# Second pass of an adaptive layer-norm block: the fourth pair's x2 is transposed by TensorE instead of by way of DRAM

## What is computed

```python
mod = (_silu(L0_c) @ L0_wmod).reshape(L0_c.shape[0], 6, 1, -1)
sa, ca, ga, sb, cb, gb = ...
h = _layernorm(x, axis=-1) * (1 + ca) + sa
x = x + ga * _L0_attn_ref(h, Wq, bq, Wk, bk, Wv, bv, Wo, bo)   # linear attention, 16 heads, elu + 1
h = _layernorm(x, axis=-1) * (1 + cb) + sb
x = x + gb * _L0_ffn_ref(h, ...)                              # value product + top 2 of 8 experts
return x                                                      # (1, 8192, 512), float32
```

## Time and profile before

| | us |
|---|---|
| runs, median of 3 (lowest to highest) | 1178.81 (1178.62 to 1179.45) |
| the profiled execution, its own time | 1178.39 |
| its span, first to last instruction | 1176.7 |
| PE busy / DVE / ACT / POOL | 1162.5 / 980.8 / 539.0 / 602.0 |
| granted TensorE clock, mean | 1.000 |

### The profile page before, as it was taken

One profiled execution on the slowest core, in us unless ns is written; L12 is line 12 of the kernel. 1 busy time (PEld: TensorE's weight loads), 2 busy tenths in 40 slices (PEclk: granted clock), 3 DMA queues, 4 the chain that ended last, 5 costly groups with the idle time before them and its releaser, 6 DMA issues.

```text
span 1176.7 us, 18181 instructions
## 1 busy us (share of the span) xinstructions
PE 1162.5 (99%) x5456; PEld 968.6 (82%) x5456; DVE 980.8 (83%) x2242; ACT 539.0 (46%) x1095; POOL 602.0 (51%) x458
## 2 busy tenths in 40 slices
PE   8999999999999999999999999999999999999998
PEld 5888888888887888888787788888888888888886
DVE  6998798888888988886788888888888888888875
ACT  4555545455445455545453443534435344344441
POOL 1444343433433433343564766666666666676632
PEclk9999999999999999999999999999999999999999
DMA  6566544543433434444313444443544534445321
GB/s 229 168 191 184 164 142 146 152 135 117 128 114 117 134 114 134 121 134 134 99 53 120 149 155 133 146 154 123 163 146 135 167 127 143 151 137 161 114 85 54
DMA packets 168834, 161.01 MB, mean 137 GB/s; under 512 B 16712, under 2 KB 115440, under 8 KB 168736
## 3 DMA queue, kind: packets, MB, share of 16 engines
q1 hardware_dynamic: 168736, 159.85, 43.6%
HBM read 95.30 MB, written 64.49 MB: 136 GB/s over the span
## 4 chain that ended last, share of the span: by engine, by line
PE 88%; DVE 4%; issue 2%; POOL 2%; ACT 2%; DMA 1%; SPq 0%; POOLq 0%; ACTq 0%; DVEq 0%
PE ps L1742 28%; PE ps L1743 28%; PE ps L1749 28%; PE ps L1963 1%; PE ps L1955 1%; POOL cn L759 1%; DMA wm_in<-in_L_wmod_dram 1%; PE ps L1850 1%; DMA q_in<-q_scratch 1%; PE ps L1761 0%; PE ps L1913 0%; PE ps L1918 0%; PE ps L1970 0%; DVE b2st L1282 0%; DVE b2st L1281 0%
## 5 line engine op out<-in xcount | busy, mean ns | idle before, releaser
L731 POOL TENSOR_TENSOR xn_lo<-xn,xn_hi 128x512 fp32r<-128x512 f32 x64 | 86.0, 1344 | 277.6 <-ACT xn_hi L866 277.6
L747 POOL TENSOR_TENSOR qks<-q_in,ks_q 128x1024 f32<-128x1024 f32 x32 | 76.9, 2403 | 103.6 <-DVE ws L1581 86.2
L759 POOL TENSOR_TENSOR cn<-c,half 128x16 f32<-128x16 f32 x32 | 93.6, 2926 | 36.9 <-DVE c L1499 36.9
L928 ACT CAST xT_hi<-ps 128x512 fp32r<-128x512 f32 x64 | 36.9, 577 | 154.3 <-DVE ps L1472 142.6
L875 ACT ACTIVATE exp_q<-qf 128x512 f32<-128x512 f32 x64 | 40.5, 633 | 141.1 <-DVE qf L1370 140.9
L1742 PE MATMUL ps<-wk_hi,xT_hi 128*128 128x512 f32 x256 | 100.4, 392 | 1.5 <-ACT xT_hi L860 1.4
L1742 PE MATMUL ps<-k_hi,xn_hi 128*128 128x512 f32 x256 | 101.9, 398 | 0.0
L1742 PE MATMUL ps<-wq_hi,xT_hi 128*128 128x512 f32 x256 | 101.3, 396 | 0.1
L1742 PE MATMUL ps<-g_hi,qT_hi 128*128 128x512 f32 x256 | 100.3, 392 | 0.1
L1742 PE MATMUL ps<-v_hi,xT_hi 128*128 128x512 f32 x256 | 100.2, 391 | 0.0
L1749 PE MATMUL ps<-k_hi,xn_lo 128*128 128x512 f32 x256 | 99.8, 390 | 0.0
(11 more groups left out here) (251 smaller groups left out, 3207.8 us busy)
## 6 DMA issues: line engine op xcount, KB each, us to landing
xin<-_attn_hidden_states_dram SPq DMA_DIRECT2D x64, 256.0 KB, 3.2
q_scratch<-qf SPq DMA_DIRECT2D x64, 256.0 KB, 3.3
xin<-_attn_hidden_states_dram SPq DMA_DIRECT2D x32, 512.0 KB, 4.3
q_in<-q_scratch SPq DMA_DIRECT2D x128, 128.0 KB, 3.0
out_dram<-qf SPq DMA_DIRECT2D x64, 256.0 KB, 2.3
xn_scratch<-xn SPq DMA_DIRECT2D x62, 256.0 KB, 2.0
xq<-xn_scratch SPq DMA_DIRECT2D x248, 64.0 KB, 2.5
x_scratch<-xn SPq DMA_DIRECT2D x56, 256.0 KB, 2.3
```

What stands on the lines that cost most here:

```text
L731: nc.gpsimd.tensor_tensor(moved(xn_lo[:, 1 - s, :], i + 1), kept(xn[:, 1 - s, :], i + 1), moved(f32(xn_hi[:, 1 - s, :]), i + 1), ALU.subtr ...
L747: nc.gpsimd.tensor_tensor(qks[:].rearrange("p h (g f) -> p (h g) f", f=P), q_of(j).rearrange("p (n f) -> p n f", f=P), ks_q[:].unsqueeze(1 ...
L759: nc.gpsimd.tensor_tensor(cn[:].rearrange("p h e -> p (h e)"), c2[:].rearrange("p h e -> p (h e)"), half[:], ALU.pow).then_inc(cn_done, 1)
L928: nc.scalar.copy(xT_hi[:, h, :], bank_x2T).then_inc(x2Th_done, 1)
```

## The change

`FIRST_TURNED` becomes 4, so that pair 3 is transposed by TensorE, and the way through DRAM begins with pair 4. The counts in the waits that had the 3 in them as a number are written with FIRST_TURNED, and the hand-written `turned_x2(3, 0)` on VectorE goes out. `turn_x2(3, 0)` and `turn_x2(3, 1)` appear on TensorE through `by_pe`; `normalised(3, ·)` writes `xn` without regrouping; SyncE's two stores and eight loads of pair 3 go out.

```diff
-        FIRST_TURNED, LAST_TURNED = 3, J - 2
+        FIRST_TURNED, LAST_TURNED = 4, J - 2
...
             def x2_load(j, h):
-                sp.wait_ge(x2_out[h], 16 * (j - 2))
-                wait_count(sp, x2T_turned, 2 * (j - 4) + h + 1)
+                sp.wait_ge(x2_out[h], 16 * (j - FIRST_TURNED + 1))
+                wait_count(sp, x2T_turned, 2 * (j - FIRST_TURNED - 1) + h + 1)
...
             def turned_x2(j, h):
-                dve.wait_ge(x2_back[h], 64 * (j - 2))
+                dve.wait_ge(x2_back[h], 64 * (j - FIRST_TURNED + 1))
...
             scores(2)
-            turned_x2(3, 0)
             weights(2)
             x2T_low(3, 0)
```

## The result

| | before | changed |
|---|---|---|
| runs, median of 6 each (lowest to highest), us | 1178.63 (1178.20 to 1179.45) | 1184.58 (1183.74 to 1185.06) |
| the profiled execution, its own time | 1178.39 | 1183.74 |
| its span | 1176.7 | 1182.0 |
| granted TensorE clock, mean | 1.000 | 0.997 |

The ratio is 1.0048, with a 95% interval of 1.0038 to 1.0058: slower by 5.9 us. The forecast was 1184.8 us. The profiled execution of the changed kernel is the quickest of its six.

The account below looks back on a forecast made before the run. TensorE's queue was taken to bound the kernel: −4.32 + 0.90 + 7.02 = +3.60 us, +6.0 with the restart, on 1178.39 is 1184.4, and 0.4 for the median gives 1184.8 us. Range 1181.9 to 1186.2.

Parts of the forecast that it names:

- The bound: TensorE, busy 1162.5 of 1176.7 us: the kernel ends when its queue of work and waits is done.
- The old stall: TensorE's delay at pair 3's products, where the transposed x2 came late by DRAM: all 4.32 us would go.
- The lower bound of 3.5: Least gain expected at pair 3's products, in us, as some delay might come back behind the new wait.
- Eight transposes: Pair 3's transposes added to TensorE's queue: 0.45 us a half, +0.90 us in all.
- The wait: TensorE at turn_x2(3, 1) waits for VectorE's x2T_low(3, 0), behind scores(2) and weights(2): +7.02 us.
- The restart: Matmuls behind TensorE's 7 us rest run slowly at first: +2.4 us, with 0 and 3.0 as ends.
- The sum: −4.32 + 0.90 + 7.02 = +3.60 us, and +6.0 with slow matmuls after the rest.
- The clock that stays up: TensorE has the same 7 us wait but no slow matmuls behind it: +3.6, 1182.4 us; chance 0.26.
- VectorE not held: VectorE's 128x32 operation slips in ahead of GpSimd's addition: wait 4.8, sum +1.4, 1180.2 us; chance 0.07.
- TensorE that hardly waits: x2T_low(3, 0) is done in time, so bank 2 is free: −3.2, 1175.6 us; chance 0.04.
- The lateness: Pair 4's DRAM way or pair 3's router is late too: further stall of 1 to 4 us, 1186 to 1189; chance 0.05.

Follow-up runs that it names:

- dram_reordered: Kernel before, pair 3 still through DRAM, with VectorE's turned_x2(3, 0) moved ahead of scores(2) and x2T_low(3, 0) ahead of weights(2); 1177.43 us.
- low_first: Changed kernel with x2T_low(3, 0) moved on VectorE from behind weights(2) to ahead of variances(2); 1176.87 us, the second time 1176.55.
- filled: Changed kernel with 30 needless 128x128 products on TensorE ahead of turn_x2(3, 1), filling its wait; 1182.45 us.
- add_later: Changed kernel with GpSimd's 128x1024 addition biased_x(4) moved from behind router_scale(2) to behind q_times_ks(6); 1181.88 us.
- turn_later: Changed kernel with turn_x2(3, 1) moved on TensorE from ahead of out_product(4, 0) to behind fused_product(3, 0); 1177.44 us.
- The second set: The changed kernel run again with no edit, in a new profile; 1184.04 us against 1179.05 for the kernel before.

## Why the prediction was right

*The bound.* TensorE's queue sets the end. Every kernel's median moved by its distance from `turn_hidden(1)` to `turn_hidden(3)`, within 0.5 us, with the one exception of +0.8 told above. Right.

*The old stall, −4.32 us.* It went in full: the second stretch is back at 18.23, and no wait is left at pair 3's products. Right in the changed kernel. The reason given for it, that the block transpose of half 0 stood behind `scores(2)`, carries only part of it: with that order changed, dram_reordered gives 1.6 of the 4.3 back. For the rest, with the waits of half 1 in it, no experiment names the reason. Nor is it all slow first matmuls that the list of waits leaves out: the run-out before each wait belongs to it, as low_first's stops show. In low_first, 1.5 of it came back, because TensorE was early again. The lower bound of 3.5 was argued for the wrong kernel: behind a 7 us stall nothing could come back.

*Eight transposes, +0.90.* 0.45 for half 0 by the trace; for half 1 it is hidden in the restart, and in filled it is 647.72 − 647.02 − 0.23 = 0.47. Right.

*The wait, +7.02.* 6.84 and 6.90 were recorded as idle; counted as in the prediction, from where the next matmul would have started without the wait (638.89 + 0.91, the usual length of four of 512 columns), it is 646.80 − 639.80 = 7.00; filled, where only the wait and the transposes are left, came out at 44.45 − 40.78 = +3.67 by the distance and +3.49 by the medians, against the +3.60 of the sum without the restart. The reason was right in each link: GpSimd's hold (add_later), the place behind `scores(2)` and `weights(2)` (low_first), and the queue behind the wait (turn_later). One number in it was short: the ready work behind the wait was not 5.4 us but 6.6, with the high part of `fused_product(3, 0)`.

*The restart, +2.4.* The mechanism was right. The size was too large for the profiled executions, which lost 1.5 to 1.7 us; by the medians it is 1.5 to 2.5. The start of the program, from which the 2.5 was taken, has the slow pace for all of its 4.64 us, and by the pace of filled's products the loss there is 4.64 − 20 x 0.114 = 2.4. In the changed kernel the slow work lasted only from 646.80 to about 649.9. The rule of the Trainium skill that spoke against the change, that a gap in the matmuls puts the clock back ("TensorE: Matmul & The Clock Gate", "Why this matters for your kernels"), is borne out: the granted clock fell to 0.50 in the long wait of all three profiles that have one (two of the changed kernel, one of add_later), and stayed at 1.00 in the profiles of the kernels without one. The argument against it, that the clock column says 1.00 even at the start, was no argument.

*The sum.* By the traces it is −4.32 + 0.90 + 7.0 + 1.6 = +5.2, and the forecast said +6.0. That the median of +5.95 met it so closely is in part luck: the restart was 0.8 too large for the execution that was profiled, and the first set of runs lay 0.8 above what its trace explains. The second set, +4.99, did not. Whether the executions without a trace lost more in the restart is open.

*The rivals.* The clock that stays up (0.26) is the kernel filled: 1182.45 where 1182.4 was worked out. VectorE not held is add_later: 1181.9, inside the 1180.2 "or up to 2 more with a slow restart". TensorE that hardly waits is low_first: 1176.9 where 1175.6 was worked out, the 1.5 that came back being missing from that sum. The lateness did not spread.

## What to carry to other kernels

When a step moves to another engine's queue, look for the semaphore it waits for there, find the operation that raises it in the other engine's order, and count what stands ahead of it; then move that operation up along with the step. A wait in an in-order queue costs as much of its length as there is ready work behind it that could have run in that time: the same late operation made TensorE wait 6.8 us with 6.6 us of ready work behind the wait, and 0.2 us with that work ahead of it. And where a busy TensorE is made to rest, count the restart as well: after rests of 4.7 and 6.9 us it cost about 1.6 in the traces, and more in some executions.

## What was not expected

- In the three profiles the loss of the restart hardly differs: 1.6 us over filled after a rest of 4.71 us (9.29 − 7.71), 1.5 and 1.7 after 6.84 and 6.90. Yet three of add_later's ten executions, at a lower mean clock, took 1.0 us more than the other seven. One profile does not give the price of a restart; the times and mean clocks of several executions do.
- At the start of the program the granted clock is given as 1.00, though the same instruction takes 0.232 us there and 0.11 in filled. Where the column shows a fall, the pace falls with it (0.43 instead of 0.23 for 512 columns); where the program begins, column and pace disagree.
- GpSimd's 128x1024 addition holds a 128x32 operation of VectorE until the addition ends: 2.32 us beside 2.34 where the two start together, and 0.36 in dram_reordered, where VectorE comes to it at 642.47 and the addition ends at 642.78. So a short operation beside it has to be priced with what is left of GpSimd's instruction. The block transpose, which reads one tensor, took 0.73 us at 641.84, within the same addition, and 0.72 without one beside it in the kernel before (644.01).
